# Second layer rows and mixture scatters written to the output tensor, empty slots left out by a bound

## The reference, cut to what matters

```python
h = h + _L1_attn_ref(_layernorm(h), ...)
# _L1_ffn_ref on x = layernorm(h):
scores = softmax(xf @ w_router.T)
_, top_idx = top_k(scores + expert_bias, 2)
top_s = top_s / (sum(top_s) + 1e-09)          # shares of the two experts
comb = zeros((T, e)).at[arange(T)[:, None], top_idx].add(top_s)
acc = acc + c[:, None] * _swiglu(xf, wg, wu, wd)   # for each of 8 experts
out = routed + _swiglu(xf, sg, su, sd)
h = h + out
```

## Time and profile before

| | |
|---|---|
| Median of 3 runs | 4409.71 us (4407.69 to 4420.83) |
| The profiled execution's own time | 4417.4 us |
| Its span, first to last instruction | 4415.7 us |
| Mean granted clock of TensorE | 0.934 of full speed |
| PE busy over the span | 3907.1 us (88%) |
| POOL busy over the span | 1333.3 us (30%) |
| Patches to attend (first instruction of project's DVE after them) | to about 3341 us |
| Project | to about 3630 us |
| Dispatch | about 3631 to 3828 us |
| Mixture | about 3828 to 4392 us |
| Output | about 4392 to 4415 us |

### The profile page before, as it was taken

The page is one execution under the profiler, slowest core; times in us unless marked ns, Lnnn a source line. Parts: engine busy times, 40 slices in busy tenths (PEclk is TensorE's granted clock), DMA queues, the critical chain, the costliest instruction groups (busy, mean ns, idle before and its releaser), DMA issues. The chain is left out here.

```text
span 4415.7 us, 74709 instructions
## 1 busy us (share of the span) xinstructions
PE 3907.1 (88%) x23896; PEld 2372.0 (54%) x23898; DVE 2477.4 (56%) x4583; ACT 1494.8 (34%) x2982; POOL 1333.3 (30%) x1520
## 2 busy tenths in 40 slices
PE   8899778799999997665999999999995989899996
PEld 8788445466666665331333333333333765577774
DVE  1576468422222222886877778777853547644443
ACT  0222124211111111342677777777771221111110
POOL 0222013244444443564001000001102121177774
PEclk9999999899999998775899999999996879999998
DMA  6221111332232221345333322233305431277776
GB/s 222 64 63 53 32 40 44 97 63 62 62 62 62 62 62 29 110 142 116 47 50 53 56 45 45 45 46 56 55 9 137 122 97 42 77 174 174 173 173 152
DMA packets 336020, 361.74 MB, mean 82 GB/s; under 512 B 50460, under 2 KB 297203, under 8 KB 334191
## 3 DMA queue, kind: packets, MB, share of 16 engines
q1 hardware_dynamic: 252255, 274.75, 25.4%
q0 software_dynamic: 61312, 63.66, 9.4%
q10 hardware_dynamic: 22288, 20.93, 1.5%
HBM read 247.51 MB, written 117.00 MB: 83 GB/s over the span
## 5 line engine op out<-in xcount | busy, mean ns | idle before, releaser
L2096 DVE TENSOR_REDUCE at_mx<-psum 128x1 f32<-128x998 f32 (+1 forms) x768 | 885.1, 1190 | 257.7 <-PE psum L1921 257.2
L2051 ACT ACTIVATE at_p<-psum 128x512 f32<-128x512 f32 (+3 forms) x1536 | 851.8, 588 | 303.4 <-PE psum L1995 273.6
L1995 PE MATMUL psum<-at_q,at_k 99*128 99x512 bf16 (+3 forms) x1536 | 522.4, 383 | 22.0 <-issue 16.9
L1921 PE MATMUL psum<-at_k,at_q 96*128 96x512 bf16 (+3 forms) x1536 | 476.0, 393 | 70.5 <-POOL at_identb L1878 32.9
L1981 PE MATMUL psum<-at_p,at_v 128*32 128x486 f32 (+3 forms) x3072 | 408.4, 604 | 1.0 <-ACT at_p L2051 0.7
L1893 POOL DMA_DIRECT2D o_rows<-at_o x96 | 48.7, 507 | 1150.0 <-DVE at_mx L2096 833.0
L1256 ACT ACTIVATE ex_silu<-psum 128x384 f32<-128x384 f32 (+1 forms) x288 | 131.8, 457 | 767.4 <-PE psum L1200 637.6
L1995 PEld LDWEIGHTS psum<-at_q,at_k 99*128 99x128 bf16 (+1 forms) x1536 | 155.7, 102 | 429.1 <-ACT at_p L2051 272.0
L1287 DVE TENSOR_TENSOR ex_hT<-ex_silu,psum 128x384 f32<-128x384 f32 (+1 forms) x288 | 147.6, 513 | 415.2 <-ACT ex_silu L1256 270.3
L1222 PE MATMUL psum<-ex_wd,ex_hT 128*128 128x192 f32 (+1 forms) x1728 | 291.5, 327 | 0.0
L1921 PEld LDWEIGHTS psum<-at_k,at_q 96*128 96x128 bf16 (+1 forms) x1536 | 151.8, 105 | 234.1 <-DVE at_mx L2096 64.0
(11 more groups left out here) (386 smaller groups left out, 7128.2 us busy)
## 6 DMA issues: line engine op xcount, KB each, us to landing
mx_wd<-in_e_dT SPq DMA_DIRECT2D x72, 288.0 KB, 4.0
qk_parts<-hd_parts SPq DMA_DIRECT2D x32, 579.4 KB, 3.7
at_k<-qk_parts SPq DMA_DIRECT2D x144, 128.8 KB, 5.3
at_q<-qk_parts SPq DMA_DIRECT2D x144, 124.8 KB, 4.7
tok_p<-in_x SPq DMA_DIRECT2D x12, 1176.0 KB, 22.7
mx_wg<-in_e_gT SPq DMA_DIRECT2D x72, 192.0 KB, 2.5
mx_wu<-in_e_uT SPq DMA_DIRECT2D x72, 192.0 KB, 2.9
v_rows<-hd_v_out SPq DMA_DIRECT2D x8, 1536.0 KB
```

Of the source, the lines that this page charges most:

```text
L1921: mm = pe.matmul(psum[0:ctx_rows[t], 3 + 2 * ((PRO + n) % 2) + k, 0:w], Q[v][0:R6, j * 1024 + 128 * t:j * 1024 + 128 * t + ctx_rows[t]], K ...
L1995: pe.matmul(psum[0:n, i % RING, 0:w], K[u][:, j, 128 * t:128 * t + n], Q[u][:, j * 1024 + at:j * 1024 + at + w], start=True, stop=True).th ...
L2051: act.activation(P[0:n, c % 2, j, 0:w], psum[0:n, i % RING, 0:w], ACT.Exp).then_inc(exp_ready, 1)
L2096: dve.tensor_reduce(mx[0:ctx_rows[t], j * CT + t:j * CT + t + 1], pair(n)[0:ctx_rows[t], 0:CTX], AX_X, ALU.max).then_inc(s_free, 1)
```

## The change

There is no `h4` and no `phase_output` any more. `build` gives the phases a view of the output tensor as 8240 rows. The views `y_img` of project and dispatch lose the offset of 256 rows, and POOL's DMA that zeroed `h4`'s pad rows is gone. Dispatch writes a second list of row numbers, `slots_out`: the row without the offset of 256, and for a slot without a row that number plus 4 x 8240, by two more DVE instructions. The mixture gathers by the old list and scatters by the new one, and the scatter has a bound of 8239 past which a row number is left out and is no error.

```diff
@@ phase_project, phase_dispatch
-        y_img = y[PAD:PAD + TOK].rearrange("(b n p) d -> b p n d", b=B, p=T)
+        y_img = y.rearrange("(b n p) d -> b p n d", b=B, p=T)
@@ phase_dispatch
+        rows_out = sb("di_rows_out", [128, NSL])
...
             pool.dma_start(xg[0:PAD].rearrange("(t p) d -> p t d", p=128), zero[:]).then_inc(pads_out, 16)
-            pool.dma_start(y[0:PAD].rearrange("(t p) d -> p t d", p=128), zero[:, :, 0:D]).then_inc(pads_out, 16)
...
-            pool.wait_ge(pads_out, 32)
+            pool.wait_ge(pads_out, 16)
...
             then(dve.scalar_tensor_tensor(out=rows[:], in0=LISTS[:, 0:NSL], scalar=128.0, in1=low_part[:],
                                           op0=ALU.mult, op1=ALU.add))
+            ordered()
+
+            then(dve.scalar_tensor_tensor(out=rows_out[:], in0=no_token[:], scalar=4.0 * TOK, in1=rows[:],
+                                          op0=ALU.mult, op1=ALU.add))
+            ordered()
+            then(dve.tensor_scalar(ids_out, rows_out[:], -float(PAD), None, ALU.add))
             then(dve.tensor_tensor(no_token[:], no_token[:], padrow[:], ALU.mult))
             ordered()
             then(dve.tensor_tensor(ids, rows[:], no_token[:], ALU.add))
@@ phase_mixture
                     pool.indirect_dma_start(y, bass.IndirectOffsetOnAxis(ap=to[:, r, t:t + 1], axis=0),
-                                            ys[:, r, t, :], None, compute_op=ALU.add).then_inc(added, 16)
+                                            ys[:, r, t, :], None, compute_op=ALU.add,
+                                            bounds_check=TOK - 1, oob_is_err=False).then_inc(added, 16)
...
-                here = ids[:, bass.ds(c * GS, GS)]
+                here = ids_out[:, bass.ds(c * GS, GS)]
                 dve.tensor_tensor(to[:, r, :], here, here, ALU.bitwise_or).then_inc(to_ready, 1)
@@ build
-    h4 = nc.dram_tensor("h4_rows", (PAD + TOK, D), F32, kind="Internal").ap()
+    rows_out = out.rearrange("b n d -> (b n) d")
...
-        slots = sb("slot_rows", [128, NSL], I32)[:]
+        slots, slots_out = sb("slot_rows", [128, NSL], I32)[:], sb("slot_rows_out", [128, NSL], I32)[:]
...
-        phase_output(nc, h4, out)
-def phase_output(nc, h4, out):
...
-        @block.sync
-        def _(sp):
-            src, dst = h4[PAD:PAD + TOK].rearrange("(b n) d -> b (n d)", b=B), out.rearrange("b n d -> b (n d)")
-            for b in range(B):
-                sp.dma_start(dst[b:b + 1].rearrange("a (p n) -> (a p) n", p=80), src[b:b + 1].rearrange("a (p n) -> (a p) n", p=80)) \
-                    .then_inc(out_stored, 16)
-            sp.wait_ge(out_stored, 16 * B)
```

More of the change, by code:

```diff
@@ L2686, in _, with phase_dispatch @@
             steps(FUSED - 1, False)
-def phase_dispatch(nc, psum, inp, h3, x3T, logits, y, xg, ids, chunk_expert, chunk_hot, ident, ident_in, consts, consts_in):
+def phase_dispatch(nc, psum, inp, h3, x3T, logits, y, xg, ids, ids_out, chunk_expert, chunk_hot, ident, ident_in,
+                   consts, consts_in):
     N = NTC * B
@@ L3105, in _, with phase_mixture @@
             ordered()
-def phase_mixture(nc, psum, inp, xg, y, ids, chunk_expert, chunk_hot, ident, ident_in):
+def phase_mixture(nc, psum, inp, xg, y, ids, ids_out, chunk_expert, chunk_hot, ident, ident_in):
     FC = F1 // 128
@@ L3434, in build @@
             logits = late.enter_context(nc.sbuf_tensor("logits", [128, NTC * B, E1], F32))[:]
-            phase_project(nc, psum, inp, o_rows, recips, y, h3, h4, x3T, logits, xg3, ident, ident_in, project, project_in,
+            phase_project(nc, psum, inp, o_rows, recips, y, h3, rows_out, x3T, logits, xg3, ident, ident_in, project, project_in,
                           dispatch, dispatch_in)
-            phase_dispatch(nc, psum, inp, h3, x3T, logits, h4, xg3, slots, chunk_expert, chunk_hot, ident, ident_in,
-                           dispatch, dispatch_in)
-        phase_mixture(nc, psum, inp, xg3, h4, slots, chunk_expert, chunk_hot, ident, ident_in)
-        phase_output(nc, h4, out)
-def phase_output(nc, h4, out):
[L3445 to L3448, removed]
-        @block.sync
-        def _(sp):
-            src, dst = h4[PAD:PAD + TOK].rearrange("(b n) d -> b (n d)", b=B), out.rearrange("b n d -> b (n d)")
-            for b in range(B):
-                sp.dma_start(dst[b:b + 1].rearrange("a (p n) -> (a p) n", p=80), src[b:b + 1].rearrange("a (p n) -> (a p) n", p=80)) \
-                    .then_inc(out_stored, 16)
-            sp.wait_ge(out_stored, 16 * B)
+            phase_dispatch(nc, psum, inp, h3, x3T, logits, rows_out, xg3, slots, slots_out, chunk_expert, chunk_hot,
+                           ident, ident_in,                           dispatch, dispatch_in)
+        phase_mixture(nc, psum, inp, xg3, rows_out, slots, slots_out, chunk_expert, chunk_hot, ident, ident_in)
 def prepare(inputs):
```

## The result

The changed kernel takes 4390.59 us (median of 5 runs, 4387.17 to 4396.76), the kernel before, over 5 runs by now, 4414.44 (4407.69 to 4420.83). The ratio is 0.9949, with a 95% interval of 0.9935 to 0.9963: 22.5 us less by the ratio, with 16 to 29 in the interval; the two medians lie 23.9 apart. The forecast was 4387.1, that is -22.6. The profiled execution took 4396.76 us, its span 4395.1.

The account below looks back on a forecast made before the run. PE was taken to bound the mixture, and only DMAs the uncovered output copy at the end. -23.3 - 0.8 + 0.7 + 0.8 = -22.6 takes the median from 4409.7 to 4387.1 us, range 4380 to 4408.

Parts of the forecast that it names:

- The output phase: At the kernel's end, the uncovered copy to the output and its frame go: -23.3 us.
- The stores to another tensor: The rows' first stores from SP go to the output tensor, same DMAs and sizes: costed at nothing.
- rival of later landings at the output: Mixture scatters land 1.13 us later at the output tensor, costing 39 us: 4426 us, chance 0.05.
- The pad rows' DMA: At dispatch's start, zeroing leaves POOL's queue, so copies and PE start sooner: -0.8 us, or 0 if DVE's chain is later.
- The two DVE instructions: At the end of dispatch, on the path, they lengthen the stretch from 0.56 to 1.22 us: +0.7.
- The bound: On the mixture's 144 scatters on POOL: 0.4 us per chunk, hidden under 0.56 of slack, so 68 chunks cost nothing.
- x: POOL time a bound adds to each mixture scatter: taken as 0.2 us, range 0 to 0.59.
- dear rival: Each mixture scatter's check on POOL costs 0.59 us, making the kernel slower: 4431 us, chance 0.12.
- The tail: Behind PE's last product, the last two chunks' scatters add 0.8 us; sooner landings taken at nothing, up to 3.9 less.
- slower rival: Mixture scatters' bound costs POOL 0.59 us each, 42 us over 68 chunks plus 2.4 at the end: 4431, chance 0.12.
- loop through the landing: In the mixture, a scatter waits for the previous chunk's landing: landing plus 2.78 us, slack 0 to 1.13, taken as 0.56.
- loop through POOL's queue: POOL's shortest mixture chunk, read where it had been held up: 6.59 us, leaving 0.84 of PE's 7.43.

Follow-up runs that it names:

- copy_gone: The kernel before with its output phase left out, only 16 rows written to the output, no bound: 4398.43 us, ratio 0.9949 to the kernel before.
- after_again: The changed kernel run again, unaltered, beside the others on the same chip: 4401.33 us, ratio 0.9953 to the kernel before.
- all_out: The changed kernel with every row number past the bound, so no scatter moves a row: 4398.55 us, ratio 0.9944 to the kernel before.
- bound_only: The changed kernel with bound and second list kept, but internal tensor and copy back restored: 4423.34 us, ratio 1.0002 to the kernel before.
- drain_early: The changed kernel with SP waiting for three phases' last landings instead of POOL, and pad-row zeroing behind dispatch's first two copies: 4391.04 us, ratio 0.9946.
- pool_plus6: The changed kernel with six more small POOL instructions per chunk ahead of its scatters: 4398.49 us, ratio 0.9964 to the kernel before.
- pool_plus10: The changed kernel with ten more small POOL instructions per chunk ahead of its scatters: 4435.61 us, ratio 1.0038 to the kernel before.

## Why the prediction was right, and where it wasn't

The mechanism was right: a phase with nothing to cover it goes, and nothing takes its place. That the sum meets the ratio's 22.5 us to 0.1 is luck. The terms as the traces have them are -22.9 - 0.5 + 0.6 - 1.6 = -24.4, and the interval of the measurement is 13 us wide.

- **The output phase**, taken at -23.3: the rest of the span is 22.9 us shorter, and copy_gone alone has the whole change's gain within the noise. The outer clearing took 0.4 us longer in this profile (and in after_again and all_out), which is the difference; without it, in copy_gone, it is 23.2.
- **The stores to another tensor**, taken at nothing: the project phase shows nothing for it at equal clock, and bound_only and copy_gone leave a few us at most. The rival of later landings at the output fell: the chunks' landings have a median of 4.24 us after the change, 4.19 before.
- **The pad rows' DMA**, taken at -0.8: 0.5 on PE's start. **The two DVE instructions**, taken at +0.7: +0.61. Dispatch is 197.7 and 197.8 us, which agrees with the two cancelling but doesn't show it: the phase spreads over 3.5 us in the table, and drain_early's PE start, 1.4 us sooner still, left it at 197.7. Whether PE's start there is worth anything stays open.
- **The bound**, taken at x = 0.2: 0, for rows that are written and for rows that are dropped. If each row's check is made by itself, as the dear rival had it, 128 of them don't show (1593 ns with the bound, 1595 without). The forecast's cost was hidden but in the tail, where it had +0.8.
- **The tail**: the forecast took no gain for dropped rows, with 3.9 as the other end. It was 2 x 0.8 = 1.6 us, so with x = 0 this term is off by 2.4 us, the largest miss of the sum. The Trainium skill (DMA: Bandwidth & Descriptors, Anatomy of one DMA — SWDGE (gpsimd) path) has a fixed time that is mostly the receipt of the write. The trace agrees in part: of 1.96 us behind POOL's part 1.1 stay when each row's packet has 8 bytes instead of 768, and 0.8 go.
- **The slower rival's price was wrong**, though the forecast did not hang on it. The step that failed is the loop through the landing, "the landing plus 2.78", with a slack of 0.56. The 2.78 held 0.52 us of issue time ahead of the scatter, which is 0.16 once POOL is late, so taking it as fixed counted slack as work; and landings came sooner when POOL was late (3.92 us in the median of pool_plus6, 3.54 in pool_plus10). The loop through POOL's queue, read from the late chunk as 6.59, was the true limit, measured at 6.50. With it x = 0.59 costs (1.18 - 0.93) x 68 = 17 us and 2.4 in the tail: an estimate of 4406, not 4431. Why landings come sooner then stays open.

## What to carry to other kernels

A phase that only moves finished rows cost its whole length here, with barriers and clearing; where the producers can write to the last place themselves, all of that goes, and the trace of before gave the sum to a microsecond. A bound on an indirect scatter's rows was free here (1593 ns against 1595). It shrinks the packet of a row past it from 768 to 8 bytes, but saves none of POOL's time. To price a threat to an engine near its limit, look for a moment when it was late and read how fast it catches up: that stretch (6.59 us) told the slack, while an ordinary stretch hides it in waits and issue time.

## What was not expected

Scatters whose rows are all past the bound still take POOL 1592 ns, while in the first layer one of 6 rows takes 0.2 us less than one of 128; so POOL's time went by the list's length and not by the bytes that are moved. It fits that a packet of 8 bytes is left of each dropped row. And POOL's drain at the end of a block is 4.80, 4.47 and 7.00 us for 288, 284 and 216 indirect DMAs, counted from the end of POOL's last DMA instruction on if nothing holds it back: it does not wait for the landing, so a wait in front of it is added in full.
